# Statistics of x taken group by group between the normalisations, at the heads of two layers of a perceiver kernel

## What is computed

```python
def _layernorm(x, axis=-1, eps=1e-05):
    m = jnp.mean(x, axis=axis, keepdims=True)
    v = jnp.var(x, axis=axis, keepdims=True)
    return (x - m) / jnp.sqrt(v + eps)

x = x + _L0_ffn_ref(_layernorm(x), ...)      # 8 experts, each token goes to one
x = x + _L1_xattn_ref(_layernorm(x), ctx_1024, ...)
x = x + _L1_attn_ref(_layernorm(x), ...)
x = x + _L1_ffn_ref(_layernorm(x), ...)      # 8 experts, each takes its 256 best tokens
x = x + _L2_xattn_ref(_layernorm(x), ctx_1024, ...)
```

## Time and profile before

| | |
|---|---|
| median of 3 runs | 3562.82 us (3559.78 to 3569.31) |
| profiled execution | 3566.51 us, its span 3564.7 us |
| mean granted TensorE clock | 0.952 |
| PE busy | 3224.8 us (90%) |
| DVE busy | 2200.5 us (62%) |
| ACT busy | 1308.8 us (37%) |
| POOL busy | 1140.9 us (32%) |

### The profile page before, as it was taken

The page is one execution under the profiler, slowest core; times in us unless marked ns, Lnnn a source line. Parts: engine busy times, 40 slices in busy tenths (PEclk is TensorE's granted clock), DMA queues, the critical chain, the costliest instruction groups (busy, mean ns, idle before and its releaser), DMA issues.

```text
span 3564.7 us, 93169 instructions
## 1 busy us (share of the span) xinstructions
PE 3224.8 (90%) x39254; PEld 2674.3 (75%) x39254; DVE 2200.5 (62%) x5259; ACT 1308.8 (37%) x3224; POOL 1140.9 (32%) x1809
## 2 busy tenths in 40 slices
PE   7988659988997969999999889989999999998996
PEld 5866447547985758888888667768888878887894
DVE  5756643356675156666666577764444458887557
ACT  5643101333222224444444443333222346665221
POOL 6767134122013443333333343200000035554003
PEclk9999779999997989999999989999999999999997
DMA  5620357541003431111111100022112111111000
GB/s 166 200 70 4 109 192 243 176 134 50 3 25 113 91 85 49 50 47 49 47 47 42 57 2 2 3 68 95 59 60 71 65 49 50 50 50 61 3 3 28
DMA packets 211279, 246.58 MB, mean 69 GB/s; under 512 B 19412, under 2 KB 191184, under 8 KB 207920
## 3 DMA queue, kind: packets, MB, share of 16 engines
q1 hardware_dynamic: 203376, 230.39, 20.6%
q0 software_dynamic: 7488, 10.23, 1.6%
HBM read 221.51 MB, written 18.61 MB: 67 GB/s over the span
## 4 chain that ended last, share of the span: by engine, by line
PE 74%; DVE 12%; issue 6%; POOL 3%; ACT 3%; DMA 1%; SPq 0%; ACTq 0%; POOLq 0%; DVEq 0%
PE psum L189 44%; PE psum L3685 11%; PE psum L971 2%; PE psum L3935 2%; PE psum L955 2%; PE psum L3144 2%; PE psum L3245 1%; PE psum L3213 1%; PE psum L3925 1%; DVE l2a_ss L1662 1%; DVE g_xn L1669 1%; POOL l0a_ms L1180 1%; PE psum L3154 1%; PE psum L594 1%; DVE g_xn L258 1%
## 5 line engine op out<-in xcount | busy, mean ns | idle before, releaser
L245 POOL TENSOR_SCALAR g_rs<-g_mv 128x4 f32<-128x4 f32 x24 | 5.0, 210 | 771.2 <-DVE g_mv L378 770.7
L3685 PE MATMUL psum<-l2f_hhi,l2f_whi 128*128 128x512 f32 x512 | 199.3, 389 | 0.0
L3685 PE MATMUL psum<-l2f_hlo,l2f_whi 128*128 128x512 f32 x512 | 199.2, 389 | 0.0
L3685 PE MATMUL psum<-l2f_hhi,l2f_wlo 128*128 128x512 f32 x512 | 199.2, 389 | 0.0
L189 PE MATMUL psum<-l2x_kT,l2x_Qp 128*128 128x257 f32 x768 | 179.1, 382 | 2.7 <-ACT g_xn L3568 2.6
L3739 DVE CAST l2f_hhi<-l2f_tmp 128x512 fp32r<-128x512 f32 x96 | 41.0, 427 | 201.7 <-ACT l2f_tmp L3802 200.6
L189 PEld LDWEIGHTS psum<-l2x_kT,l2x_Qp 128*128 128x128 f32 x768 | 141.9, 191 | 21.9 <-issue 3.3
L3802 ACT ACTIVATE l2f_tmp<-psum,g_cols 128x512 f32<-128x512 f32 x64 | 44.2, 690 | 240.1 <-PE psum L3685 240.1
L3568 ACT ACTIVATE g_xn<-psum,l2x_sm 128x257 f32<-128x257 f32 x192 | 88.8, 472 | 90.7 <-DVE l2x_sm L3474 90.7
L4132 ACT ACTIVATE l3x_P<-psum,l3x_sm 128x257 f32<-128x257 f32 x256 | 117.6, 479 | 2.7 <-DVE l3x_sm L4054 2.7
L389 DVE TENSOR_TENSOR g_x<-g_x,psum 128x256 f32<-128x256 f32 x128 | 53.2, 416 | 99.1 <-PE psum L189 96.4
(11 more groups left out here) (890 smaller groups left out, 10632.8 us busy)
## 6 DMA issues: line engine op xcount, KB each, us to landing
l2f_raw<-L2f_h SPq DMA_DIRECT2D x64, 512.0 KB, 3.3
l0f_w<-L0f_w SPq DMA_DIRECT2D x23, 1024.0 KB
l0x_ctxT<-ctxT SPq DMA_DIRECT2D x64, 257.0 KB, 2.8
l1x_ctxT<-ctxT SPq DMA_DIRECT2D x64, 257.0 KB, 5.6
l0x_ctok<-ctx SPq DMA_DIRECT2D x64, 256.0 KB, 3.4
l1x_ctok<-ctx SPq DMA_DIRECT2D x64, 256.0 KB
l2x_cT<-ctxT SPq DMA_DIRECT2D x64, 256.0 KB, 2.8
l2x_tok<-ctx SPq DMA_DIRECT2D x128, 128.0 KB, 2.9
```

The lines of the kernel that those rows point to most:

```text
L3685: t = e.matmul(z, a, b, start=c == 0 and u == 0, stop=c == 7 and u == 2)
```

## The change

The statistics of x move from the end of the two routed layers into the head of the next layer. `Norm` is told the four signals of the groups' landing (`landed`), and DVE's pipeline gets a first stage, `spread`, which waits for a group's landing and takes its four tiles' statistics. `apply` moves to lag 1 and `evict` to lag 2. DVE's order at the two heads becomes S0, S1 A0, S2 A1 E0, S3 A2 E1, A3 E2, E3, where it was S0 S1 S2 S3, A0, A1 E0, A2 E1, A3 E2, E3. POOL's wait for `stat` now counts from the beginning of the layer. The signals `x_back` become lasting ones. The other layers have `landed` unset, and their order stays as it is.

```diff
@@ class Norm
-    def __init__(self, K, second=None, first=False):
+    def __init__(self, K, second=None, landed=None):
@@ def pool
-            w.wait_ge(K.sig("stat").at(4 * g + 4 if self.first else 4 * g - 12))
+            w.wait_ge(K.sig("stat").at(4 * g + 4 if self.landed else 4 * g - 12))
@@ def dve
-        if self.first:
-            for i in range(16):
-                statistics(K, e, w, i)
+
+        def spread(g):
+            if self.landed:
+                w.wait_ge(self.landed[g].at(0))
+                for i in range(4 * g, 4 * g + 4):
+                    statistics(K, e, w, i)
...
-        ticks(4, {0: apply, 1: evict}, [0, 1])
+        ticks(4, {0: spread, 1: apply, 2: evict}, [0, 1, 2])
@@ def l0_ffn (and the same in l1_ffn)
-        ... back_in = ..., [L(f"x_back{g}") for g in range(4)]
+        ... back_in = ..., [K.gathered(f"x_back{g}") for g in range(4)]
+        K.landed = back_in
...
-            for i in range(16):
-                w.wait_ge(back_in[i // 4].at(1))
-                statistics(K, e, w, i)
@@ def l1_xattn
-        norm, mark, order = Norm(K), {}, [9, 8, 7, 6, 5, 4, 3, 2, 1, 0]
+        norm, mark, order = Norm(K, landed=K.landed), {}, [9, 8, 7, 6, 5, 4, 3, 2, 1, 0]
@@ def l2_xattn
-        norm = Norm(K, second=(1e-5, K.col("L2_xattn_vid_g"), K.col("L2_xattn_vid_b")))
+        norm = Norm(K, second=(1e-5, K.col("L2_xattn_vid_g"), K.col("L2_xattn_vid_b")), landed=K.landed)
```

More of the change, by code:

```diff
@@ L209 @@
     EPS = 1e-5
-    def __init__(self, K, second=None, first=False):
+    def __init__(self, K, second=None, landed=None):
         S = K.sig
-        self.K, self.second, self.first = K, second, first
+        self.K, self.second, self.landed = K, second, landed
         self.rs, self.xn, self.ps, self.dv, self.ac = S("ln_rs"), S("ln_xn"), S("ln_turned"), S("ln_xT_dve"), S("ln_xT_act")
@@ L1906, in l0_ffn @@
         Y = [T(f"y{k}", [128, 256]) for k in range(4)]
-        wt, xs_in, sum_in, back_in = L("weights"), L("xs_in"), L("sum_in"), [L(f"x_back{g}") for g in range(4)]
+        wt, xs_in, sum_in, back_in = L("weights"), L("xs_in"), L("sum_in"), [K.gathered(f"x_back{g}") for g in range(4)]
+        K.landed = back_in
         w_in, x_in, added = [L(f"w{k}_in") for k in range(6)], [G_(f"gathered{k}") for k in range(8)], [G_(f"added{k}") for k in range(4)]
@@ L2620, in l1_ffn @@
         hT, yf = [T(f"hT{k}", [128, 6, 256]) for k in range(2)], [T(f"yf{k}", [128, 256]) for k in range(4)]
-        wt, xs_in, sum_in, added, back_in = L("weights"), L("xs_in"), L("sum_in"), K.gathered("scattered"), [L(f"x_back{g}") for g in range(4)]
+        wt, xs_in, sum_in, added, back_in = L("weights"), L("xs_in"), L("sum_in"), K.gathered("scattered"), [K.gathered(f"x_back{g}") for g in range(4)]
+        K.landed = back_in
         w1_in, w2_in, x_in = [L(f"up_in{k}") for k in range(2)], [L(f"down_in{k}") for k in range(3)], [K.gathered(f"gathered{k}") for k in range(4)]
```

## The result

The changed kernel takes 3573.75 us (median of 16 runs, 3563.63 to 3579.03), the kernel before on the same chip 3564.11 us (16 runs, 3557.91 to 3572.76). The ratio is 1.0018 with an interval of 1.0010 to 1.0027, that is 3.6 to 9.6 us slower. The forecast was +3.3 us, 3566.1, with a range of 3558 to 3574. The sign, the mechanism and the class (within 0.3%) came out as forecast. The size did not: it is about twice the forecast by the ratio (6.4 us), and nearly three times by the two medians (9.6 us).

What follows compares the result with a forecast made beforehand. TensorE, busy 90% of the span, was taken as the bound, with VectorE on the path at L1's and L2's cross-attention heads. Terms of +2.1 and +1.2 us on 3562.8 gave 3566.1 us, range 3558 to 3574.

Steps and rivals of the forecast that it cites:

- Waits for POOL: In L1's and L2's cross-attention heads, normalisations A0 to A2 stall for POOL's reciprocals: +0.85 us each head, bounds 0.4 and 1.2.
- The wait that goes: At L2's cross-attention head, DVE no longer waits for group 2 of x: -0.57 us.
- Neighbours at site 1: At L1's cross-attention head, POOL's memsets and copies stretching normalisations: no change, bounds -0.6 and +0.5 us.
- At site 2 forecast -0.4: At L2's cross-attention head, POOL's memsets hold one DVE instruction instead of two: -0.4 us, bounds -0.9 and +0.3.
- The clock: In both cross-attention heads, spread transposes delay PE's full clock: +1.29 us each, bounds 0 and 2.0.
- The tail: In both heads, last normalisation to first matmul runs at half clock: +0.56 us each.
- The dense products at half clock: Behind both heads' transposes, 2.9 us of dense matmuls at half clock lose 1.45; half taken, +0.73 us each.
- Sum: L1's cross-attention head +2.1 us, L2's +1.2, together +3.3, bounds -1.3 and +6.6.
- The second: In both heads PE's clock keeps its old course, only waits and neighbours count: +0.7 us, 3563.5; chance 0.24.
- The third: Half clock persists through L1's cross-attention projections: undetectable below 21 us of it, all 60 us giving 3600 us; chance 0.03.
- The fourth: In the heads, A0 waits beyond group 1 and the old order returns, or DVE's order matters elsewhere: 3562.8 us; chance 0.02.
- the fifth: The two heads' stretches yield a kernel faster by over 0.3%, 10.7 us; chance 0.01.

Runs made afterwards that it cites:

- e9: Kernel before, old order, no added products, with GpSimd's fills and copies held behind the last normalisation at four attention heads; 3559.79 us, ratio 0.9976.
- e7: Changed kernel with unit-matrix products keeping PE busy and POOL's preparations held until the last normalisation, in both heads; ratio 0.9991 to the kernel before.
- e3: Changed kernel with normalisations and evictions one group later (S0 S1 S2 A0 S3 A1 E0 A2 E1 A3 E2 E3); 3569.86 us, ratio 1.0007.
- e4: Changed kernel with idle PE kept busy in both heads by 16, 8 and 10 unit-matrix products ahead of transpose groups; 3562.09 us, ratio 0.9983.
- e10: Kernel before's order (all statistics first) with 13 unit-matrix products on idle PE ahead of the first transpose in both heads; ratio 0.9990.
- e6: Changed kernel with POOL's memsets, copies and tables in the two heads held until the last normalisation, no added products; ratio 1.0018 to the kernel before.
- e8: e7 with fills also held at L0's and L3's attention heads, ScalarE's copy of v waiting for its own buffer only; 3558.99 us, ratio 0.9974.
- e2: The change at L2's cross-attention head alone, L1's head as in the kernel before; 3573.28 us, ratio 1.0014.
- e1: The change at L1's cross-attention head alone, L2's head as in the kernel before; 3571.93 us, ratio 1.0010.

## Why the prediction was right or wrong, step by step

1. *Waits for POOL, 0.85 a site: right.* Measured are 0.28, 0.24 and 0.10 to 0.18 for A0, A1 and A2 (forecast 0.35, 0.31 and 0.19). The releaser is L247, A3 waits for none, and the first transposes came 4.0 us after the first statistics (3.5 forecast, 6.9 before). At site 1 the last normalisation ends 14.88 us after the first statistics, against 13.47: of these 1.41 the neighbours are 0.56, which leaves 0.85. With clock and neighbours removed, e9 against e7 gives 0.84.
2. *The wait that goes, -0.57 at site 2: right.* It is gone in the changed kernel, and back (0.66) in e3, where S2 is issued ahead of A0 again. q in e4 lies 0.46 below e10, where the forecast's terms give 0.85 - 0.57 - 0.4 = -0.12: at this site the waits came out smaller (the last normalisation ends 0.45 sooner, which with -0.57 and -0.55 leaves 0.67 for them) and the neighbours' gain larger.
3. *Neighbours at site 1, forecast 0 with bounds of -0.6 and +0.5: mis-sized, and just outside its bounds.* Normalisations took 1.38 x 3 + 2.49 = 6.63 against 2.98 + 1.37 + 1.72 = 6.07, so +0.56; A3 alone lost 1.12, which e6 and e7 gave back. I spread POOL's work over A3 by what it had cost before; it is 3.0 us long (604.21 to 607.16), and moving the normalisations later laid the longest undisturbed row of it, the four copies, exactly over the last one. Before, two of the four copies ran 600.42 to 601.82 and the other two, late for their data, 603.07 to 604.31, so A3 from 603.71 on met only 0.6 us of them. The forecast also read the 0.24 lost by the first eight as the cost of the `pow`, which e9 shows to cost nothing; it was the same memsets and copies. The step that was missing is to add up POOL's queue from its new start and lay it over the one instruction left. At site 2 forecast -0.4; measured 1.38 x 3 + 1.90 = 6.04 against 3.66 + 1.56 + 1.37 = 6.59, -0.55.
4. *The clock: the mechanism right, the size off by more than two.* This is the failed term: 1.29 a site was forecast, 3.46 and 2.36 were measured in the two heads. The tail was forecast at 0.56 and is 0.55 at site 1 and 0.54 at site 2. The dense products at half clock were forecast at half of 1.45, 0.73; they cost 2.91 and 1.82. Two choices were wrong. I took half of the effect because I doubted it, and both sites had it in full. And I carried over 2.9 us of half clock from the earlier trace rows, where here the rise came 5.9 and 3.7 us into the products. Both sites lie above the upper bound of 2.0. A further 1.31 at site 2 lie behind q, where the forecast had nothing. The Trainium skill ("TensorE: Matmul & The Clock Gate", "Part 1: The HAM clock gate") has activity release the throttle; the runs agree in direction, with the rise at 615.3 behind spread transposes and at 604.3 behind packed ones.
5. *Sum.* Forecast +2.1 and +1.2. Up to Q and q the sites lost 4.89 and 1.94: the clock 3.46 and 2.36, the order at full clock +1.43 and -0.46. At the markers behind they lost 5.09 and 3.26, together 8.35, more than the forecast's own upper sum of 6.6. The measured median, 3573.75, lies 0.25 below the upper end of the range. It is inside because the range had been widened by the spread of the runs, and not because the bounds of the clock were good: that was luck.
6. *Rivals.* The second, a clock that keeps its course, fell at both sites. The third, half clock throughout the projections, did not come: it lasted 5.9 us of some 60. The fourth fell by the traces, and the fifth by the measured time.

**What stays open.** e4 and e9 are faster by more than their heads, and e7, e8 and e10 may be, within their intervals. e4 is 4.5 us below before by the medians, 3 to 9 by the ratio's interval, with heads that add 1.28. Over all its runs PE's mean clock was 0.956, against 0.952 for before in the same comparison; twice the missing part times the span is 314 us at half clock against 345, 31 fewer. In the profiled pair the difference is some 22 us (mean clocks 0.955 and 0.952), and the two heads account for 16 of them: the 30 us from the first statistic of site 1 and the 60 from that of site 2 hold 33.0 us of half clock before and 16.8 in e4. Where the rest of the 31 comes from I can't show. Other stretches with the same code differ between kernels too: from 400 to 500 us there are 82 us of half clock before, 80 in e4, 76 in the changed kernel and 72 in e2, e9 and e10, and I found no instruction behind it. Within the 35 runs of before the time rises by 0.3 us for each us at half clock, so 15 fewer would be 4 to 5 us, the size of what is missing. That is a correlation, not a test. It is also open what starts the further spell of half clock behind site 2's head.

## What to carry to other kernels

When work is moved between an engine that feeds TensorE and TensorE's first dense work, look at how TensorE's small work is packed just ahead of it: transposes that were packed had raised the clock in time, and spreading them cost 3.5 and 2.4 us in the two heads, where waits and neighbours came to +1.4 and -0.5. Starting the consumer earlier is worth nothing where it waits for the last group anyway. And look for memory fills that run beside VectorE's critical normalisations: holding GpSimd's fills at four heads, with the order left alone, went with a kernel 5 to 13 us faster, of which 4.9 are seen in two of the heads. A fill that is needed soon behind the head gives part of it back.

## What the runs showed that I had not expected

- After transposes with pauses of 0.92 and 1.50 us the clock stayed at half through 3.7 us (site 2) and 5.9 us (site 1) of dense products; after packed ones it rose ahead of them. With the same order it rose 13.9 or 16.7 us after the first statistic of site 2 (before, e1).
- A `tensor_scalar` of 128x256 takes 0.34 us alone (1.37 for four), 0.62 on average beside GpSimd's copies (2.49), and up to 0.6 beside its memsets (2.38), but still 0.33 beside the small `pow` (2.65 for eight in e9, the whole `pow` of 1.20 us beside them). The Trainium skill ("SBUF — State Buffer", "Who interferes with whom") says that VectorE and GpSimd share a pair of SBUF ports; the fills and copies agree with it, the `pow` doesn't show it.
- The fills lose as well: ten of 128x512 took 5.85 us beside normalisations and 4.73 when held, four of 128x1024 4.16 and 3.62.
